# Self-attention maxima in four groups instead of fifteen single products, and the second batch's normalization moved ahead

## The reference, cut to what matters

```
x = x + tanh(g_xattn[0]) * cross_attention(layernorm(x), ctx, mask)      # layer A, 16 heads, 77 keys
x = x + tanh(g_ffn[0])   * top2_moe(layernorm(x)) + shared expert         # layer B
x = x + tanh(g_xattn[1]) * cross_attention(layernorm(x), ctx)             # layer C, 16 heads, 77 keys
x = x + tanh(g_ffn[1])   * self_attention_ffn(layernorm(x))               # layer D
```

## Time and profile before

| | |
|---|---|
| time, median of 3 | 272.37 us (271.57, 272.37, 278.62) |
| the profiled execution | 271.53 us |
| its span, first to last instruction | 269.7 us |
| mean granted TensorE clock | 0.994 |
| PE busy | 243.5 us, 90% of the span |
| DVE busy | 116.1 us, 43% |
| ACT busy | 100.4 us, 37% |
| POOL busy | 86.4 us, 32% |

### The profile page before, as it was taken

One profiled execution on the slowest core, in us unless ns is written; L12 is line 12 of the kernel. 1 busy time (PEld: TensorE's weight loads), 2 busy tenths in 40 slices (PEclk: granted clock), 3 DMA queues, 4 the chain that ended last, 5 costly groups with the idle time before them and its releaser, 6 DMA issues.

```text
span 269.7 us, 4272 instructions
## 1 busy us (share of the span) xinstructions
PE 243.5 (90%) x1667; PEld 130.1 (48%) x1682; DVE 116.1 (43%) x359; ACT 100.4 (37%) x160; POOL 86.4 (32%) x111
## 2 busy tenths in 40 slices
PE   7889999999877899978999869999899978999984
PEld 2334333355437668766854323334244256237652
DVE  1847336124658202011205793264527852683111
ACT  0422743674181074633300135623840048101731
POOL 2640700003335777777750306000730046000000
PEclk9979999999999999999999999999999999999999
DMA  7999000002300221211115000000000000000011
GB/s 221 403 411 367 3 0 2 0 2 67 89 1 2 49 50 48 44 41 53 38 34 156 0 0 2 0 0 2 0 4 0 0 0 2 0 0 2 2 39 39
DMA packets 10844, 14.65 MB, mean 54 GB/s; under 512 B 1335, under 2 KB 7866, under 8 KB 10826
## 3 DMA queue, kind: packets, MB, share of 16 engines
q1 hardware_dynamic: 9168, 11.29, 11.7%
q0 software_dynamic: 1280, 2.33, 3.5%
q10 hardware_dynamic: 378, 0.78, 0.9%
HBM read 10.75 MB, written 3.93 MB: 54 GB/s over the span
## 4 chain that ended last, share of the span: by engine, by line
PE 73%; DVE 10%; ACT 7%; issue 3%; DMA 3%; POOL 2%; SPq 0%; ACTq 0%; DVEq 0%; POOLq 0%
PE wk L565 13%; PE ts L836 7%; PE wk L887 6%; PE wk L663 6%; PE ts L712 5%; PE wk L738 5%; PE wk L667 3%; DVE nmx L1257 3%; PE ts L715 3%; PE wk L594 3%; PE wk L753 2%; PE wk L849 2%; DMA pk<-in_pk 2%; PE ts L702 2%; PE wk L778 2%
## 5 line engine op out<-in xcount | busy, mean ns | idle before, releaser
L565 PE MATMUL wk<-warm 128*128 128x512 bf16 x190 | 52.4, 401 | 4.4 <-DVE warm L1381 1.4
L1250 DVE TENSOR_REDUCE nmx<-wk 128x4 f32<-128x308 f32 (+1 forms) x62 | 33.2, 576 | 25.8 <-PE wk L667 19.4
L449 POOL TENSOR_TENSOR rstd<-ve,half 128x4 f32<-128x4 f32 (+1 forms) x8 | 9.7, 1209 | 94.6 <-DVE ve L1232 94.6
L565 PEld LDWEIGHTS wk<-warm 128*128 128x128 bf16 x205 | 18.9, 102 | 37.0 <-issue 9.9
L1100 ACT ACTIVATE pr<-ts 77x1024 f32<-77x1024 f32 x28 | 27.0, 1017 | 19.8 <-PE ts L715 10.3
L503 POOL DMA_INDIRECT pr<-xs_d,src_i x20 | 20.5, 1023 | 8.5 <-issue 4.3
L1167 ACT ACTIVATE pr<-ts,pk 128x320 f32<-128x320 f32 x32 | 16.6, 527 | 16.7 <-PE ts L836 16.5
L508 POOL DMA_INDIRECT y_d<-onT,dst_i x20 | 20.0, 998 | 6.5 <-issue 5.5
L887 PE MATMUL wk<-w,pr 128*128 128x128 f32 (+1 forms) x192 | 20.0, 278 | 0.0
L836 PE MATMUL ts<-pr,w 128*128 128x320 f32 x64 | 18.7, 435 | 1.3 <-ACT pr L1160 0.7
L887 PEld LDWEIGHTS wk<-w,pr 128*128 128x128 f32 (+1 forms) x192 | 18.4, 173 | 1.5 <-issue 1.2
(11 more groups left out here) (224 smaller groups left out, 374.1 us busy)
## 6 DMA issues: line engine op xcount, KB each, us to landing
w<-in_w SPq DMA_DIRECT2D x8, 512.0 KB, 11.4
y_d<-fill SPq DMA_DIRECT2D x1, 1024.0 KB, 11.6
xs_d<-xn SPq DMA_DIRECT2D x4, 256.0 KB, 2.5
y<-y_d SPq DMA_DIRECT2D x4, 256.0 KB, 3.8
pk<-in_pk SPq DMA_DIRECT2D x1, 928.0 KB, 8.4
bpk<-in_bpk SPq DMA_DIRECT2D x1, 517.0 KB, 6.7
x<-in_x SPq DMA_DIRECT2D x2, 256.0 KB, 5.5
sw<-in_sw SPq DMA_DIRECT2D x2, 256.0 KB, 7.8
```

The source lines that it names most:

```text
L565: m = pe.matmul(w, warm[:, 0:P], warm[:, :], start=True, stop=True)
L1250: v.tensor_reduce(dst, src, AX.X, ALU.max, negate=True).then_inc(job_dve, 1)
```

## The change

It touches layer D alone, and the hand-written orders around it.

- The 15 products of a batch go in four groups. A is (e, h) = (1,0), (1,1), (1,2), (3,0) in the four banks of `wk`; B is heads 0 to 3 of block 0 in the four banks of `ts`; C is (1,3), (2,0), (2,1) in three banks of `wk`; D is heads 4 to 7 of block 0 in `ts` again, after B has been taken. One semaphore step announces a group when its last product is done. DVE takes B and D with one reduction over four banks, C with one over three, A with one over three banks and one over the fourth.
- Before each group of batch 0 stand two products of ones; batch 1 has none. Two more are in jobs of their own between B and C of batch 0 (`fill`), which also bring group C to its banks.
- Group A of batch 0 stands before v's projection and the second `token_major` of layer C, B after it, C before `channel_major`, D before `project_out`.
- Batch 1: DVE's statistics move before its reduction of D of batch 0. POOL computes a shift for it, ACT normalizes it and takes the transposed batch with scale and offset, and PE's transposes of it stand before the nT transposes of batch 0, which now have six products of ones before them instead of four; the three that stood behind them are gone. q, k and v of batch 1 are made between the rounds of scores D,0, and DVE takes q and k instead of ACT. Group D of batch 1 and its wait stand between the second and third step of the values of batch 0.

```diff
-QM2 = [(e, h) for e in range(TB) for h in range(HEADS_OF[e])]
+D_MAX = {"A": [(1, 0), (1, 1), (1, 2), (3, 0)], "B": [(0, h) for h in range(4)],
+         "C": [(1, 3), (2, 0), (2, 1)], "D": [(0, h) for h in range(4, 8)]}
...
     add("act", ("pv", "C", 1, 0), ("q", "D", 0), ("k", "D", 0), ("pv", "C", 1, 1))
-    add("dve", ("tm", "C", 1, 0), ("v", "D", 0))
-    mx("D", 0, 0, 2)
-    add("dve", ("tm", "C", 1, 1))
-    mx("D", 0, 2, 6)
+    add("dve", ("tm", "C", 1, 0))
+    mxd(0, "A")
+    add("dve", ("v", "D", 0), ("tm", "C", 1, 1))
+    add("pe", ("fill", "D", 2), ("fill", "D", 3))
+    mxd(0, "C")
     add("act", ("onT", "C", 1))
-    mx("D", 0, 6, 8)
     add("dve", ("y", "C", 1))
-    mx("D", 0, 8, 15)
+    add("act", ("xT", "D", 1))
     add("dve", ("nT", "D", 0))
-    add("pe", ("fill", "D", 0))
     add("act", ("h4", 0))
     wk_round("D", 0)
-    add("dve", ("xT", "D", 1))
-    add("act", ("q", "D", 1), ("k", "D", 1))
-    add("dve", ("v", "D", 1))
-    mx("D", 1, 0, 15)
+    add("dve", ("q", "D", 1), ("k", "D", 1), ("v", "D", 1))
+    add("pe", ("fill", "D", 0))
+    mxd(1, "A")
+    mxd(1, "C")
     add("act", ("pv", "D", 0))
...
+            def maxima_d(b, g, wait_products=2):
+                n = len(D_MAX[g])
+                if g in "AC":
+                    banks = [bank("mxd", b, g, i) for i in range(n)]
+                else:
+                    banks = [ts[:, i, :] for i in range(n)]
+                    if g == "B":
+                        pe.wait_ge(s_exp, 2 * (s_index("CD"[b], 1 - b, 3) + 1))
+                    else:
+                        pe.wait_ge(mxd_out, 2 * b + 1)
+                keep_warm(banks[0], wait_products)
+                if g == "A":
+                    after("q", "D", b)
+                    after("k", "D", b)
+                for w, (e, h) in zip(banks, D_MAX[g]):
+                    j, v = h % 4, h // 4
+                    m = pe.matmul(w, qT[b][32 * j:32 * j + 32, P * e:P * e + P], kd[32 * j:32 * j + 32, b, v, :], start=True, stop=True)
+                if g in "AC":
+                    m.then_inc(job_mm, n)
+                else:
+                    m.then_inc(mxd_mm, 1)
...
             token_major("C", 1, 0)
+            maxima_d(0, "A")
             project("v", "D", 0)
-            maxima("D", 0, 0, 2)
             token_major("C", 1, 1)
-            maxima("D", 0, 2, 6)
+            maxima_d(0, "B")
+            fill("D", 2, 1)
+            fill("D", 3, 1)
+            maxima_d(0, "C")
             channel_major("C", 1)
-            maxima("D", 0, 6, 8)
+            maxima_d(0, "D")
             project_out("C", 1)
-            maxima("D", 0, 8, 15)
-            transposes_max("D", 0, 4)
-            fill("D", 0, 3)
+            transposes_x("D", 1)
+            transposes_max("D", 0, 6)
             scores_h4(0)
             scores("D", 0, 0)
             scores("D", 0, 1)
-            transposes_x("D", 1)
+            project("q", "D", 1)
             scores("D", 0, 2)
-            project("q", "D", 1)
             project("k", "D", 1)
+            project("v", "D", 1)
             scores("D", 0, 3)
-            project("v", "D", 1)
-            maxima("D", 1, 0, 15)
+            fill("D", 0, 1)
+            maxima_d(1, "A", 0)
+            maxima_d(1, "B", 0)
+            maxima_d(1, "C", 0)
             w = bank("pv", "D", 0)
-            for kt in range(TB):
-                m = values_d(w, 0, kt)
-            m.then_inc(job_mm, 1)
-            transposes_max("D", 1)
+            values_d(w, 0, 0)
+            values_d(w, 0, 1)
+            maxima_d(1, "D", 0)
+            values_d(w, 0, 2)
+            values_d(w, 0, 3).then_inc(job_mm, 1)
+            transposes_max("D", 1, 2)
...
+            def take_maxima_d(b, g):
+                heads = D_MAX[g]
+                n = len(heads)
+                if g in "AC":
+                    at = JOB["mxd", b, g, 0]
+                    v.wait_ge(job_mm, at + n)
+                    banks = wk[:, at % WKB:at % WKB + n, :]
+                else:
+                    v.wait_ge(mxd_mm, 2 * b + (1 if g == "B" else 2))
+                    banks = ts[:, :, :]
+                for lo, hi in ([(0, 3), (3, 4)] if g == "A" else [(0, n)]):
...
+                    m = v.tensor_reduce(dst, banks[:, lo:hi, :], AX.X, ALU.max, negate=True)
+                    if g in "AC":
+                        m.then_inc(job_dve, hi - lo)
                     else:
+                        m.then_inc(mxd_out, 1)
...
             divide("C", 1, 0)
+            take_maxima_d(0, "A")
             take_v2(0)
-            take_maxima("D", 0, 0, 2)
             divide("C", 1, 1)
-            take_maxima("D", 0, 2, 8)
+            take_maxima_d(0, "B")
+            take_maxima_d(0, "C")
             residual("C", 1)
-            take_maxima("D", 0, 8, 15)
+            norm_stats("D", 1)
+            take_maxima_d(0, "D")
             split_maxima("D", 0)
             take_nT("D", 0)
-            norm_stats("D", 1)
-            norm("D", 1)
-            take_xT2(1)
+            take_q2_k2()
             take_v2(1)
-            take_maxima("D", 1, 0, 15)
+            for g in "ABCD":
+                take_maxima_d(1, g)
```

More of the change, by code:

```diff
@@ L113, in mx, with mxd @@
         add("dve", *[("mx", L, b, n) for n in range(lo, hi)])
+    def mxd(b, g):
+        add("dve", *[("mxd", b, g, i) for i in range(len(D_MAX[g]))])
     def mx4(L):
@@ L205 @@
 assert all(JOB["s", L, b, 0] % 2 == 0 for L, b in WK_ROUNDS)
+assert all(JOB["mxd", b, g, 0] % WKB + len(D_MAX[g]) <= WKB for b in range(B) for g in "AC")
 def taken(n):
@@ L452, in shift_rstd @@
             def shift_rstd(L, b):
+                which = 1 if L == "D" else 0
                 own(pool.tensor_scalar(shift[:, :], mv[:, b, :, 0], -1.0, None, ALU.mult))
                 pool.wait_ge(rstd_ready, LN[L, b] + 1)
-                pool.tensor_tensor(shift[:, :], shift[:, :], rstd[:, b, 0, :], ALU.mult).then_inc(shift_ready, 1)
+                pool.tensor_tensor(shift[:, :], shift[:, :], rstd[:, b, which, :], ALU.mult).then_inc(shift_ready, 1)
             own(pool.memset(half[:, :], -0.5))
@@ L646, in maxima @@
                     after("q", L, b)
-                    after(*(("k", "D", b) if L == "D" else ("k", L)))
-                pairs = [range(n, min(n + 2, hi)) for n in range(lo, hi, 2)]
-                for pair in pairs:
+                    after("k", L)
+                for pair in [range(n, n + 2) for n in range(lo, hi, 2)]:
                     banks = {}
                     for n in pair:
+                        t = n // 4
                         banks[n] = bank("mx", L, b, n)
-                        if L != "A":
+                        if L == "C":
                             keep_warm(banks[n], 1)
                         else:
-                            t = n // 4
                             pe.matmul(banks[n][:, 0:4 * NK], mnegT[:, S * b + P * t:S * b + P * t + P], bpack("big4")[0:NK, :],
@@ L1182, in _ @@
             copy_out(oT[1][:, 0, :], "pv", "C", 1, 0)
-            take_q2(0)
-            take_k2(0)
+            act.activation(qT[0][:, :], job("q", "D", 0), ACT.Identity, bias=col("bqD")).then_inc(job_act, 1)
+            w = job("k", "D", 0)
+            act.wait_ge(hb_ready, 2)
+            for v in range(2):
+                m = act.activation(kd[:, 0, v, :], w, ACT.Identity, scale=col(f"hd{v}"), bias=hbd[:, v:v + 1])
+            m.then_inc(job_act, 1)
             copy_out(oT[1][:, 1, :], "pv", "C", 1, 1)
             copy_out(onT[1][:, :], "onT", "C", 1)
-            exp_h4(0)
[L1189 to L1194, removed]
+            normalize("D", 1)
+            w = job("xT", "D", 1)
+            act.wait_ge(xTD_zero, B)
+            for t in range(TB):
+                n = D >> t
+                m = act.activation(xTD[0:n, 1, P * t:P * t + P], w[0:n, P * t:P * t + P], ACT.Identity,
+                                   scale=col("nw")[0:n], bias=col("nb")[0:n])
+            m.then_inc(job_act, 1)
+            exp_h4(0)
+            for r in range(TB):
+                exps("D", 0, r)
             copy_out(oT[0][:, 0, :], "pv", "D", 0)
@@ L1265, in split_maxima @@
             def split_maxima(L, b):
-                if L in "AC" and b == 0:
+                if L == "D":
+                    v.wait_ge(*done("mxd", b, "C", 2))
+                    v.wait_ge(mxd_out, 2 * b + 2)
+                elif b == 0:
                     v.wait_ge(mx4_out, 2 if L == "A" else 4)
                 else:
-                    v.wait_ge(*done("mx", L, b, (len(QM2) if L == "D" else H) - 1))
+                    v.wait_ge(*done("mx", L, b, H - 1))
                 if L == "A":
```

61 lines of the change are left out of this document (26 added, 35 removed).

## The result

The changed kernel took 277.05 us (273.61 to 279.91 in 6 runs), the kernel before 272.12 beside it: a ratio of 1.016, 95% interval 1.009 to 1.022. The forecast was 272.5, within 268.3 to 276.0: the change is slower than its range allowed. The profiled execution took 277.8 us, span 276.0.

What follows compares the result with a forecast made beforehand. The pairing of PE and DVE, neither engine alone, was taken as the bound. The profiled 271.53 us + 4.7 (stage one) - 5.0 (stage two) + 1.3 (clock fall) = 272.5, range 268.3 to 276.

Steps and rivals of the forecast that it cites:

- the pairing of PE and DVE: Batch 1's maxima before the change: period 1.60 us, DVE taking a pair in 1.29, then idling about 0.31; neither engine alone bounds.
- the stage sums at full clock: Layer C's end to head 4's scores of batch 0 loses 4.7 us; from there to batch 1's scores gains 5.0.
- The waits at A and v: First stage: group A waits for DVE's division until 200.44; v then waits 1.9 us for A's three-bank reduction.
- the second pass of A's fourth product: Group A's last product needs the rows of its first, so the group takes 2.12 us on PE instead of 1.06.
- the sizes of the reductions: DVE's group reductions at 1.03 ns an element: 2.27 us for 2048 elements, 1.74 for 1536.
- the hole and its length: PE has nothing from project_out's end at 213.6 to the first normalized tile at 218.8: 5.2 us.
- x of batch 1 as the last link: End of first stage: batch 1's normalization, not the maxima, decides when scores start, 222.5 against 217.84.
- the three signs of being wrong: v does not wait; nT transposes wait for nsp, not x's transposes; DVE has gaps between batch 1's groups.
- The clock: After PE's idle of 5.2 us, one fall to 1.2 GHz over batch 1's transposes and six ones: 1.3 us more.
- the spell at 13.9: Evidence row: PE's clock fell to 1.2 GHz after 1.78 us of work in 3.40, and stayed for 3.40.
- Rival (c): Clock does not come back after 213.6, low over 9.8 us of stage two's PE work: 279.5 us; chance 0.08.
- "slower by 2%" bound: Whole kernel: two per cent is 5.4 us, about what a measurement can tell; slower had chance 0.09.

Runs made afterwards that it cites:

- e2_fill_three: Changed kernel with 22 ones ahead of batch 1's transposes, plus 4 before and 8 after group A of batch 0: ratio to the kernel before 1.0017.
- e1_fill_hole: Changed kernel with 22 products of ones in front of batch 1's transposes: ratio to the kernel before 0.9997, repeated 1.0072.
- e3_dense_after: Changed kernel with 14 instead of 6 ones between batch 1's transposes and the nT transposes: ratio to the kernel before 1.0201.
- a0_change: The changed kernel unaltered, timed again on the chip of the next runs: 278.96 us against 271.28 for the kernel before, ratio 1.0315.
- b2_ts_first_denser: Changed kernel reordered (v and both token_major first, then groups B, D, A, C), more ones in PE's waits: ratio to the kernel before 0.9821.
- experiment 5: Changed kernel, hole left, with 14 instead of 6 ones between batch 1's transposes and the nT transposes: ratio to the kernel before 1.0201.

## Why the prediction was wrong

**Right:** the bound before, the pairing of PE and DVE; the stage sums at full clock. The first stage at full clock was to take 23.56 (222.5 less 198.94) and took 23.31 in e2_fill_three, which has 12 ones in the waits around A; the second 23.6, and 23.56 in e1_fill_hole, in its repeat and in e3_dense_after. The waits at A and v, the second pass of A's fourth product, the sizes of the reductions, the hole and its length, and x of batch 1 as the last link are in the trace as forecast. That POOL's shift and the tail cost nothing held (23.2 in both). None of the three signs of being wrong came, and the clock of 0.50 behind the hole was on the list of what would show it, but without a length.

**The step that failed is the one headed "The clock":** "I expect one fall, low over the transposes and the six ones", 1.3 us. In its place the runs showed a low spell of 17.1 and 20.5 us, and another in front of it (3.4 us). By stages: the first lost 26.56 - 23.31 = 3.2 us to the clock, not 1.3. Half of that is the fall that was forecast (26.56 - 24.93 = 1.6, near enough to 1.3), the other half a fall behind the waits of 1.0 and 1.9 us around A that was not (24.93 - 23.31 = 1.6). The second lost 27.86 - 23.56 = 4.3 us (5.6 in a0_change), not 0. The miss of the profiled execution is 5.3 us (277.8 against 272.5), and these two terms are 1.9 and 4.3; against them stand an earlier start of the stage by 0.6 us (198.32 against 198.94) and 0.3 by which the first stage's own sum was too long.

The error had two roots. I took the 3.40 us of the spell at 13.9 for the length of a spell, from one case. The same stretch in b2_ts_first_denser was low for 17.1 us, so that one case gave no length. And the row that I used for comfort (1.73 us of work in 3.40 at 220.0, no fall) is one in which the clock had not fallen; it says nothing of how it comes back. The second root is that I priced the low clock over the transposes and the six ones alone, though all of stage two stands behind them. What sets the length is open: behind the fall at 13.9 stood wide and narrow products, eight of them of 32 rows, as behind the hole.

```profile
13.97 1.44 PE L565 MATMUL wk<-warm 128*128 128x512 bf16 x3 [1.13 <-DVE qT L1303]
15.21 1.23 PE L632 MATMUL wk<-bpk,mnegT 77*128 77x308 bf16 x4
16.36 1.25 PE L635 MATMUL wk<-kblkA,qT 32*128 32x308 f32 x8
```

Rival (c), that the clock does not come back, was the right mechanism with its place and its direction; it had 0.08, with a size of 7 us where 4.3 to 5.6 were found. The "slower by 2%" bound was not passed in the first comparison and was in the second.

The Trainium skill, "TensorE: Matmul & The Clock Gate", section "Why this matters for your kernels", asks both for no idle gaps between bursts and for continuous work to get back to the full rate; the first half I had used. On the first half the runs agree for the hole of 5.4 us, but the clock also fell behind the waits of 1.0 and 1.9 us around A, in all six profiles that have them. And the prediction's word that the trace agrees at 13.9 was too much: PE's longest wait before that fall was 1.13 us. On the second half experiment 5 agrees (full clock 6.8 us after the fall with a dense run, 17 without), and the spell of 17.1 us in b2_ts_first_denser, with PE busy throughout, does not; the measurement decides.

## What to carry to other kernels

Before a product of ones is removed, or a wait moved in front of PE, ask what PE does in the stretch behind it: here the price of a hole was its own length and then a clock of 1.2 GHz for 6.8 to 20.5 us; in the changed kernel that cost 4.3 and 5.6 us where the second stage had gained 5.1 at full clock. One case of a low spell is no measure of the next: price a range. When an exchange between two engines is made coarser, order the groups so that the first one needs no bank that somebody still holds; the group in the fixed banks went first in the version that won. And a clock loss does not show as idle time: compare the durations of the same instruction, or the clock column, stage by stage, before looking for a cause in the order.

## What the runs showed of the hardware that I had not expected

The granted clock stayed at 1.2 GHz for 17.1 and 20.5 us behind a hole of 5.4 us although PE was busy 71% to 100% of each stretch of the first and 58% to 100% of the second; with 8 more wide products there it was back after 6.8 us. In b2_ts_first_denser it stayed at 1.2 GHz for 17.1 us with PE busy 100% of each stretch, over products behind which it came back after 3.4 us in the kernel before. Waits of 1.0 and 1.9 us about 4 us apart were followed by a fall of 3.4 us in each profile that has them. Four float products of 32 rows in four row groups take 1.14 us, with two of them in one row group 1.98. One reduction of 2048 elements over four banks takes 2.29 us against four times 0.69.
